# Row maxima into the scores by one-hot products instead of a DMA, and bias loads on a second queue

## The chip, the core and the metric

The kernel runs on one core of a Trainium2 chip. The metric is the device time of one launch in microseconds. TensorE is PE here, VectorE DVE, ScalarE ACT, GpSimd POOL, SyncE SP (its DMA queue SPq).

## What is computed

A pre-norm decoder block over x of shape (16, 128, 128), 16 heads of 8, fp32. Three layers, each over all 16 sequences:

```python
x = x + causal_self_attention(layernorm(x))               # q = k = v, no weights
x = x + cross_attention(layernorm(x), ctx, bias)          # scores = q k^T / sqrt(8) + bias, bias (16, 16, 128, 128)
x = x + attention(hn)                                     # hn = layernorm(x) * g + b, own wq wk wv wo
x = x + top1_moe(layernorm(x) * g2 + b2)                  # 8 experts, hidden 512
```

All softmaxes are over 128 keys of the same sequence.

## The kernel before

**Blocks and slots.** One sequence in one layer is a block: b = 0 to 15 are self attention (SELF), 16 to 31 cross attention (CROSS), 32 to 47 the attention of the last layer (FFN). Two blocks are a pair, q = b // 2. Every engine runs the same loop over slots b with its own part of the work written out by hand, and counting semaphores hold the engines together. After slot 50 comes the routing of rows to experts and the expert stage (from about 490 us on), which the change doesn't touch.

**Scores.** Queries and keys are split into three bf16 parts, and the nine products of parts are stacked in the contraction: 9 x 8 = 72 rows (ROWS). That layout needs another distribution over partitions, so it goes through DRAM: `write_parts(q)` writes q once (192 KB) and k three times (576 KB), `read_stack(q)` waits for those writes and reads both operands back as `stack[:, q % 3]` (2 x 576 KB). For pair q, SP issues the write in slot 2(q-2) and the read in the slot after. The parts come by the chain PE `qk_products` (slot 2q-5), ACT `high_parts`, DVE `first_rest` (same slot), ACT `middle_parts` and POOL `low_parts` (slot 2q-4). ACT takes `middle_parts` after the first exponential of that slot.

**Row maxima.** CROSS and FFN blocks need their row maxima ahead of the exponential. Slot b makes them for block b+2: PE `score_maxes(b+2, g)` (four groups g of four heads) computes plain scores into max_bank, DVE adds the bias (CROSS) and reduces (`row_maxes`), `max_parts` makes two bf16 parts of the negated maxima, high in columns 0 to 15 and the rest of them in 16 to 31. In slot b+1 PE transposes them (`max_transposed`) and DVE copies them out as `maxT[:, b % 2, :]` (`take_maxT`). They enter the scores as two further rows of the contraction (MROWS = 74): the key side of these rows is ones, the query side is maxT, which a DMA puts there:

```python
def max_rows(b):
    wait(sp, s_maxT, b - B + 1)
    sp.dma_start(stack[ROWS:MROWS, b // 2 % NSTACK, 0, :, b % 2 * S:(b % 2 + 1) * S],
                 maxT[0:2 * NH, b % 2, :]).then_inc(s_maxrow[b % 2], 16)
```

**The order on PE in slot b** is: `scores(b, 0)`, `scores(b, 1)`, (FFN: `attention_transposed(b-2)`), `add_outputs(b-1)`, `max_transposed(b+1)`, `score_maxes(b+2, 0)` and `(b+2, 1)`, v products in even slots, `scores(b, 2)`, `out_projected(b-2)`, qk products in odd slots, `scores(b, 3)`, `out_transposed(b-1)`, `score_maxes(b+2, 2)` and `(b+2, 3)`, in even slots `transposes(q+3)`. In a CROSS block a score group is four times a transpose of the bias (fp32, into the bank) and a product on top of it.

**The order on DVE**: in even slots statistics for pair q+3, then `take_maxT(b+1)`, row maxima of groups 0 and 1 of block b+2, values, normalise, residual, `attention(b-1)`, row maxima 2 and 3, `max_parts(b+2)`. POOL computes the inverse deviation for pair q+3 before `low_parts(q+2)` in even slots.

**The order on SP**, all on one DMA queue: odd slots `read_stack(q+2)`, `load_bias(b+4)`, `max_rows(b+1)`; even slots `load_ctx(q+4)`, `load_bias(b+4)`, `max_rows(b+1)`, `write_parts(q+2)`. The biases of blocks 16 to 20 are loaded in slots 5, 7, 9, 11, 13, those of 21 to 31 in slots 17 to 27. From slot 33 on an expert weight (256 KB) goes with each slot, and a filler of 1 MB follows the writes in slots 34, 38 and 42.

Of the kernel before, what the change touches and what calls it, by code (L numbers as in the profile page):

```python
# [7 lines left out]
B, S, D = 16, 128, 128  # L8
NH, HD = 16, 8
# [4 lines left out]
G = 4  # L14
NG = NH // G
PAIR = 2 * S
NT = 3
ROWS = NT * NT * HD
MROWS = ROWS + 2
VC = 32  # L20
VS = 16
MASKED = -1e30
# [36 lines left out]
def build(nc, a, out):  # L59
# [4 lines left out]
    with ctx:  # L64
        def sb(name, shape, dt=f32):
            return ctx.enter_context(nc.sbuf_tensor(name, shape, dt))
# [15 lines left out]
        hT = sb("hT", [128, 2, PAIR])  # L82
        rest = sb("rest", [128, 2, PAIR])
        parts = sb("parts", [128, 2, NT, 2, PAIR], bf16)
        stack = sb("stack", [MROWS, NSTACK, 2, NH, PAIR], bf16)
        vaug = sb("vaug", [128, NVAUG, NH + 1, VS])
        bias_in = sb("bias_in", [128, NBIAS, NH, S])
        probs = sb("probs", [128, 2, NG, G * S])
# [8 lines left out]
        ident = sb("ident", [128, 128])  # L97
        identb = sb("identb", [128, 128], bf16)
        causal = sb("causal", [128, G, S], bf16)
        ones_row = sb("ones_row", [128, PAIR], bf16)  # L100
        zero = sb("zero", [128, 1])
        minus_half = sb("minus_half", [128, 4])
        in_block = sb("in_block", [128, TQ])
# [56 lines left out]
        s_bias = [sem(f"bias_loaded{i}") for i in range(NBIAS)]  # L160
        s_wr = [sem(f"scratch_written{i}") for i in range(2)]
        s_stack = [sem(f"stack_loaded{i}") for i in range(NSTACK)]
        s_ones = sem("ones_in_stack")
        s_maxrow = [sem(f"max_rows_in_stack{i}") for i in range(2)]
        s_pool_const = sem("pool_constants")
        s_ident = sem("identity_causal_zeros")
        s_dve_const = sem("dve_constants")
# [75 lines left out]
        def _(sp):  # L243
# [24 lines left out]
                                ap=[[row_elems, ROWS], [1, row_elems]])  # L268
                sp.dma_start(stack[0:ROWS, i, 1, :, :], k_src).then_inc(s_stack[i], 16)  # L269

            def max_rows(b):
                wait(sp, s_maxT, b - B + 1)
                sp.dma_start(stack[ROWS:MROWS, b // 2 % NSTACK, 0, :, b % 2 * S:(b % 2 + 1) * S],
                             maxT[0:2 * NH, b % 2, :]).then_inc(s_maxrow[b % 2], 16)

            def load_bias(b):
                i = b % NBIAS
                if b - NBIAS >= FIRST_CROSS:
                    sp.wait_ge(s_e, NG * (b - NBIAS + 1))
                sp.dma_start(bias_in[:, i, :, :],  # L280
                             a["bias"][b - B].rearrange("h q k -> q h k")).then_inc(s_bias[i], 16)

            def load_ctx(q):
                i, n = q % 2, 2 * q - B
                if q - 2 >= CROSS_PAIR:
# [39 lines left out]
            for b in range(NB + 1):  # L325
                q = b // 2
                if b % 2 == 1 and q + 2 < NP:
                    read_stack(q + 2)
                if 1 <= b <= 5:
                    load_weights(3 * b - 3, 3 * b)  # L330
                if b == 6:
                    sp.wait_ge(s_pool_const, 1)
                    for i in range(NSTACK):
                        sp.dma_start(stack[ROWS:MROWS, i, 1, :, :],
                                     ones_row[0:2, :].unsqueeze(1).to_broadcast([2, NH, PAIR])).then_inc(s_ones, 16)
                if b % 2 == 0 and CROSS_PAIR <= q + 4 < FFN_PAIR:
                    load_ctx(q + 4)
                if b in BIAS_AT:
                    load_bias(BIAS_AT[b])
                elif 17 <= b and b + 4 < FIRST_FFN:  # L340
                    load_bias(b + 4)
                if FIRST_CROSS <= b + 1 < NB:
                    max_rows(b + 1)
                if b % 2 == 0 and q + 2 < NP:
                    write_parts(q + 2)
                if b > FIRST_FFN:
                    load_expert(b)
                if b in (34, 38, 42):
                    write_filler((b - 34) // 4)
# [25 lines left out]
        def _(pool):  # L375
# [77 lines left out]
            low_parts(1)  # L453
            self_values(1)
            self_values(2)
            nc.gpsimd.memset(ones_row[:], 1.0).then_inc(s_pool_const, 1)
            nc.gpsimd.memset(in_block[:], 1.0).then_inc(s_pool_const, 1)
            nc.gpsimd.memset(before[:], 1.0).then_inc(s_pool_const, 1)
            nc.gpsimd.memset(filler[:], 0.0).then_inc(s_pool_const, 1)
# [1 line left out]
            def constants():  # L461
                pool.wait_ge(s_pool_const, 4)
                nc.gpsimd.affine_select(out=in_block[:], in_=in_block[:], compare_op=ALU.is_ge, fill=0.0, base=0,
                                        pattern=[[-TR, TQ]], channel_multiplier=1).then_inc(s_pool_const, 1)
                nc.gpsimd.affine_select(out=before[:], in_=before[:], compare_op=ALU.is_gt, fill=0.0, base=0,
                                        pattern=[[1, 128]], channel_multiplier=-1).then_inc(s_pool_const, 1)
                pool.wait_ge(s_pool_const, 6)
                nc.gpsimd.affine_select(out=in_block[:], in_=in_block[:], compare_op=ALU.is_ge, fill=0.0, base=TR - 1,
                                        pattern=[[TR, TQ]], channel_multiplier=-1).then_inc(s_pool_const, 1)
                nc.gpsimd.iota(expert_no[:], pattern=[[1, E]], base=0, channel_multiplier=0,  # L470
                               allow_small_or_imprecise_dtypes=True).then_inc(s_pool_const, 1)
                nc.gpsimd.iota(tile_ends[:], pattern=[[TILE, B]], base=0, channel_multiplier=0,
                               allow_small_or_imprecise_dtypes=True).then_inc(s_pool_const, 1)
                nc.gpsimd.iota(tile_no[:], pattern=[[1, NTILES]], base=0, channel_multiplier=0,
                               allow_small_or_imprecise_dtypes=True).then_inc(s_pool_const, 1)
                nc.gpsimd.iota(filler[:].bitcast(i32)[:, 2 * D:WIDTH], pattern=[[0, 1]], base=B * S,
                               channel_multiplier=1).then_inc(s_pool_const, 1)
                nc.gpsimd.iota(rows_out[:].bitcast(i32)[:, :, 2 * D], pattern=[[S, B]], base=0,
                               channel_multiplier=1).then_inc(s_pool_const, 1)

            for b in range(LAST_SLOT):
                q = b // 2
# [39 lines left out]
        def _(pe):  # L522
# [67 lines left out]

            def scores(b, g):
                i, s, bk, kind = b // 2 % NSTACK, b % 2, sbk[g % 2], layer(b)
                depth = ROWS if kind == SELF else MROWS
                wait(pe, s_p, NG * b + g - 1)
                if g == 0:
                    pe.wait_ge(s_stack[i], READS * (b // 2 // NSTACK + 1))
                    if kind == CROSS:
                        pe.wait_ge(s_bias[b % NBIAS], 16 * ((b - B) // NBIAS + 1))
                    if kind != SELF:
                        pe.wait_ge(s_maxrow[b % 2], 16 * ((b - B) // 2 + 1))  # L600
                    if b == FIRST_CROSS:
                        pe.wait_ge(s_ones, 16 * NSTACK)
                if kind == SELF:
                    mm(bk[:], identb[:], causal[:].rearrange("p g k -> p (g k)"), stop=False)
                for h in range(G):
                    o, head = bk[:, h * S:(h + 1) * S], g * G + h
                    if kind == CROSS:
                        tr(o, bias_in[:, b % NBIAS, head, :], stop=False)
                    last = mm(o, stack[0:depth, i, 1, head, s * S:(s + 1) * S],
                              stack[0:depth, i, 0, head, s * S:(s + 1) * S], start=kind == FFN,  # L610
                              stop=kind != SELF or h == G - 1)
                last.then_inc(s_e, 1)

            def add_outputs(b):
# [127 lines left out]
        def _(act):  # L742
# [42 lines left out]
            def take_hn2T(j):  # L785
                act.wait_ge(s_t, NP + j + 1)
                nc.scalar.activation(hn2T[:, j % 2, :], pb[:, 0:PAIR], ACT.Identity,
                                     bias=cols[:, 7:8], scale=cols[:, 6:7]).then_inc(s_hn2, 1)

            high_parts(0)  # L790
            middle_parts(0)
            high_parts(1)
# [3 lines left out]
            for b in range(LAST_SLOT):  # L796
                q = b // 2
                if b < NB:
                    exponentials(b, 0)
                if b % 2 == 0 and q + 2 < NP:  # L800
                    middle_parts(q + 2)
                if FIRST_FFN <= b - 2 < NB:
                    take_attT(b - 2)
                if b < NB:
                    exponentials(b, 1)
                if 0 <= b - 1 < NB:
                    take_out(b - 1)
                if b < NB:
                    exponentials(b, 2)
                if b % 2 == 1 and CROSS_PAIR <= q + 3 < NP:  # L810
                    high_parts(q + 3)
                if b < NB:
                    exponentials(b, 3)
                if b % 2 == 0 and q + 3 < NP:
                    if player(q + 3) == SELF:
                        high_parts(q + 3)
                    else:
                        take_hT(q + 3)
                if b in LAST_NORMS:
                    take_hn2T(LAST_NORMS[b])  # L820
# [27 lines left out]
        def _(dve):  # L848
# [92 lines left out]

            def take_maxT(b):
                dve.wait_ge(s_mtr, b - B + 1)
                wait(dve, s_maxrow[b % 2], 16 * ((b - B) // 2))
                nc.vector.tensor_copy(maxT[:, b % 2, :], fb[:].bitcast(bf16)[:, 0:128]).then_inc(s_maxT, 1)  # L945

            def attention(b):
# [212 lines left out]
```

## Time and profile before

| | |
|---|---|
| time, median of 3 runs | 578.4 us (578.15 to 583.85) |
| profiled execution, its time | 579.91 us |
| profiled execution, its span | 578.2 us |
| granted clock of TensorE, mean | 0.812 of 2.4 GHz |
| PE busy | 373.3 us (65%) |
| DVE, ACT, POOL busy | 291.0, 202.9, 169.9 us |
| moved by DMA | 82.35 MB, mean 142 GB/s |

The span runs from the first to the last instruction on the core. A busy share is an average over stages with different limits: self attention up to about 146 us, cross attention up to about 336, the last attention layer up to about 480, then routing and experts.

### The profile page before, as it was taken

What the parts mean: (1) busy time and instruction counts of PE and PEld (TensorE: products, weight loads), DVE (VectorE), ACT (ScalarE), POOL (GpSimd) and SP (SyncE); (2) the same over time, 40 slices, a digit from 0 to 9 for tenths busy, and PEclk for the clock granted to TensorE, in tenths of its full rate; (3) what the DMA queues carried; (4) which work ended last, traced back from release to release, by engine and by line L of the source; (5) the groups of instructions that cost most, each with busy time, mean ns of one, the idle gap of its engine ahead of it and who ended that gap; (6) DMA issues with size and microseconds to landing.
All of it is one profiled execution on the core that took longest, in us unless ns stands there. A gap on an engine that the chain in (4) does not pass through costs nothing.

```text
span 578.2 us, 11981 instructions
## 1 busy us (share of the span) xinstructions
PE 373.3 (65%) x4299; PEld 318.1 (55%) x4299; DVE 291.0 (50%) x845; ACT 202.9 (35%) x414; POOL 169.9 (29%) x244
## 2 busy tenths in 40 slices
PE   1285666625849696686958966486367395007995
PEld 0164444514638585675857856376356384007995
DVE  4124121215775575755757655545366274404773
ACT  1255444422324232332324333344245163003552
POOL 4222101210122222333334544123123123371543
PEclk9989777777787897987979977857788588557999
DMA  2777677888384856758544433945856421122331
GB/s 76 187 191 201 173 196 214 217 217 215 99 202 128 214 139 174 199 135 217 130 105 116 116 81 103 227 108 131 203 158 156 103 84 47 36 104 68 100 88 39
DMA packets 75335, 82.35 MB, mean 142 GB/s; under 512 B 6171, under 2 KB 61566, under 8 KB 71822
## 3 DMA queue, kind: packets, MB, share of 16 engines
q1 hardware_dynamic: 73774, 78.43, 52.8%
q0 software_dynamic: 1504, 3.16, 1.6%
q8 instruction: 35, 0.57, 0.4%
q14 instruction: 22, 0.18, 0.1%
HBM read 56.20 MB, written 25.51 MB: 141 GB/s over the span
## 4 chain that ended last, share of the span: by engine, by line
DMA 36%; PE 25%; SPq 18%; DVE 10%; issue 5%; POOL 4%; ACT 0%; POOLq 0%; DVEq 0%; ACTq 0%
DMA stack<-maxT 21%; DMA k_scratch<-parts 12%; PE out_bank L524 7%; PE score_bank L524 5%; SPq L257 5%; PE proj_bank L524 4%; PE score_bank L527 3%; PE max_bank L524 3%; SPq L287 3%; POOL routed_rows L507 3%; SPq L266 2%; DVE biased L920 2%; DVE rowmax L924 2%; SPq L253 2%; SPq L269 2%
## 5 line engine op out<-in xcount | busy, mean ns | idle before, releaser
L773 ACT ACTIVATE probs<-score_bank 128x512 f32<-128x512 f32 x192 | 112.2, 598 | 220.4 <-PE score_bank L524 218.7
L524 PE MATMUL score_bank<-stack 74*128 74x128 bf16 (+1 forms) x768 | 111.2, 247 | 49.8 <-DMA stack<-maxT 49.8
L524 PEld LDWEIGHTS score_bank<-stack 74*128 74x128 bf16 (+1 forms) x768 | 74.3, 113 | 64.9 <-issue 57.4
L527 PE MATMUL score_bank<-ident,bias_in 128*128 128x128 f32 x256 | 57.6, 309 | 35.9 <-DMA stack<-maxT 35.9
L524 PE MATMUL out_bank<-probs,vaug 128*32 128x128 f32 x1536 | 68.9, 336 | 0.0
L527 PEld LDWEIGHTS score_bank<-ident,bias_in 128*128 128x128 f32 x256 | 41.1, 161 | 42.1 <-issue 36.1
L429 POOL TENSOR_TENSOR att_sel<-att,in_block 128x1024 f32<-128x1024 f32 x16 | 34.3, 2144 | 89.7 <-DVE att L956 89.7
L524 PEld LDWEIGHTS out_bank<-probs,vaug 128*32 128x32 f32 x1536 | 50.6, 134 | 10.4 <-issue 5.0
L524 PE MATMUL score_bank<-causal,identb 128*128 128x512 bf16 x64 | 29.8, 465 | 40.9 <-DMA stack<-k_scratch 40.9
L381 POOL TENSOR_SCALAR vareps<-meanvar 128x2 f32<-128x2 f32 x32 | 7.1, 223 | 164.4 <-DVE meanvar L869 164.3
L945 DVE COPY maxT<-finish_bank 128x128 bf16<-128x128 bf16 x32 | 7.1, 222 | 93.4 <-PE finish_bank L589 93.4
L920 DVE TENSOR_TENSOR biased<-max_bank,bias_in 128x512 f32<-128x512 f32 x64 | 43.7, 683 | 18.0 <-PE max_bank L524 17.0
L524 PE MATMUL max_bank<-stack 72*128 72x128 bf16 x512 | 44.7, 237 | 12.2 <-DMA stack<-k_scratch 12.2
L950 DVE RECIPROCAL rowsum_inv<-finish_bank 128x16 f32<-128x16 f32 x48 | 12.2, 255 | 68.0 <-PE finish_bank L527 68.0
L924 DVE TENSOR_REDUCE rowmax<-biased 128x4 f32<-128x512 f32 x64 | 43.9, 686 | 2.2
L394 POOL TENSOR_TENSOR parts<-rest,parts 128x512 bf16<-128x512 f32 (+1 forms) x24 | 23.9, 995 | 70.5 <-ACT parts L768 70.5
L524 PEld LDWEIGHTS max_bank<-stack 72*128 72x128 bf16 x512 | 37.0, 107 | 13.2 <-DMA stack<-k_scratch 12.7
L929 DVE TENSOR_REDUCE rowmax<-max_bank 128x4 f32<-128x512 f32 x64 | 41.5, 682 | 1.6 <-PE max_bank L524 1.4
L779 ACT COPY outT<-out_bank 128x512 f32<-128x512 f32 x48 | 28.1, 586 | 29.1 <-PE out_bank L524 29.0
L524 PEld LDWEIGHTS score_bank<-causal,identb 128*128 128x128 bf16 x64 | 7.0, 109 | 46.3 <-issue 44.9
L514 POOL DMA_INDIRECT out<-vaug x23 | 22.6, 982 | 32.4 <-DVE vaug L1120 30.4
L524 PE MATMUL proj_bank<-wxo,att_sel 128*128 128x128 f32 x256 | 32.0, 278 | 0.0
(141 smaller groups left out, 642.5 us busy)
## 6 DMA issues: line engine op xcount, KB each, us to landing
k_scratch<-parts SPq DMA_DIRECT2D x72, 192.0 KB, 3.2
stack<-q_scratch SPq DMA_DIRECT2D x24, 576.0 KB
stack<-k_scratch SPq DMA_DIRECT2D x24, 576.0 KB
q_scratch<-parts SPq DMA_DIRECT2D x24, 192.0 KB, 2.9
bias_in<-in_w SPq DMA_DIRECT2D x16, 256.0 KB, 3.9
routed_rows<-filler SPq DMA_DIRECT2D x2, 1028.0 KB, 8.9
vaug<-routed_rows SPq DMA_DIRECT2D x23, 64.5 KB, 1.8
parts<-routed_rows SPq DMA_DIRECT2D x23, 64.0 KB, 2.1
```

The source lines that it names most:

```text
L257: sp.dma_start(k_rows, parts[:, i, part, wk, :].unsqueeze(1).to_broadcast([128, NT, PAIR])).then_inc(s_wr[i], 16)
L287: sp.dma_start(ctx_in[:, i, :, :], a["ctx"][n:n + 2].rearrange("b s d -> s b d")).then_inc(s_ctx[i], 16)
L394: nc.gpsimd.tensor_tensor(parts[:, i, 2, 0:n, :], rest[:, 0:n, :], parts[:, i, 1, 0:n, :], ALU.subtract).then_inc(s_lo, 1)
L429: nc.gpsimd.tensor_tensor(att_sel[:], att[:, b % 2, :].rearrange("p (h d) -> p d h", d=HD).unsqueeze(3).to_broadcast([128, HD, NH, TQ]), i ...
L514: nc.gpsimd.indirect_dma_start(out=out.rearrange("b s d -> (b s) d"), out_offset=bass.IndirectOffsetOnAxis(ap=tile_res[:, buf, :].bitcast( ...
L524: return nc.tensor.matmul(o, lhsT, rhs, start=start, stop=stop, **kw)
L527: return nc.tensor.matmul(o, src, ident[:], start=True, stop=stop, is_transpose=True)
L773: nc.scalar.activation(probs[:, b % 2, g, :], sbk[g % 2][:], ACT.Exp, scale=1.0 if layer(b) == CROSS else SCALE).then_inc(s_p, 1)
L779: nc.scalar.copy(outT[:], ob[:]).then_inc(s_out, 1)
L920: nc.vector.tensor_tensor(biased[:, u % 2, :], bk[:], bias_in[:, b % NBIAS, g * G:(g + 1) * G, :].rearrange("p h k -> p (h k)"), ALU.add). ...
L924: nc.vector.tensor_reduce(rowmax[:, g * G:(g + 1) * G], biased[:, u % 2, :].rearrange("p (h k) -> p h k", h=G), AX.X, ALU.max).then_inc(s_ ...
L929: nc.vector.tensor_reduce(rowmax[:, g * G:(g + 1) * G], bk[:].rearrange("p (h k) -> p h k", h=G), AX.X, ALU.max).then_inc(s_mfree, 1)
```

## The change

The two further rows leave the stack, and with them `max_rows`, the ones, and their semaphores. A constant `pick` (bf16, 128 x 16 x 128) has ones in rows h and 16 + h of head h. A product of `pick[:, head, :]` with `maxT` (contraction over 128) adds both parts of the negated maxima of that head to every key; it follows each score product of CROSS and FFN blocks, 16 to a block. PE now waits for maxT itself. DVE's copy of maxT, which waited for the DMA, now waits for the scores of the block two before, the last readers of its buffer. The bias loads move from SP to ACT, in the same slots, behind the slot's first exponential.

```diff
-MROWS = ROWS + 2
-        stack = sb("stack", [MROWS, NSTACK, 2, NH, PAIR], bf16)
+        stack = sb("stack", [ROWS, NSTACK, 2, NH, PAIR], bf16)
-        ones_row = sb("ones_row", [128, PAIR], bf16)
+        pick = sb("pick", [128, NH, S], bf16)
...
@@ sync: max_rows, load_bias, the ones and their calls go
-                if b == 6:
-                    sp.wait_ge(s_pool_const, 1)
-                    for i in range(NSTACK):
-                        sp.dma_start(stack[ROWS:MROWS, i, 1, :, :],
-                                     ones_row[0:2, :].unsqueeze(1).to_broadcast([2, NH, PAIR])).then_inc(s_ones, 16)
-                if b in BIAS_AT:
-                    load_bias(BIAS_AT[b])
-                elif 17 <= b and b + 4 < FIRST_FFN:
-                    load_bias(b + 4)
-                if FIRST_CROSS <= b + 1 < NB:
-                    max_rows(b + 1)
@@ gpsimd
-            nc.gpsimd.memset(ones_row[:], 1.0).then_inc(s_pool_const, 1)
+            nc.gpsimd.memset(pick[:], 0.0).then_inc(s_pool_const, 1)
...
+                nc.gpsimd.affine_select(out=pick[:], in_=pick[:], compare_op=ALU.not_equal, fill=1.0, base=0,
+                                        pattern=[[-1, NH], [0, S]], channel_multiplier=1).then_inc(s_pool_const, 1)
+                pool.wait_ge(s_pool_const, 13)
+                nc.gpsimd.affine_select(out=pick[:], in_=pick[:], compare_op=ALU.not_equal, fill=1.0, base=-NH,
+                                        pattern=[[-1, NH], [0, S]], channel_multiplier=1).then_inc(s_pool_const, 1)
@@ tensor, scores(b, g)
                     if kind != SELF:
-                        pe.wait_ge(s_maxrow[b % 2], 16 * ((b - B) // 2 + 1))
+                        pe.wait_ge(s_maxT, b - B + 1)
                     if b == FIRST_CROSS:
-                        pe.wait_ge(s_ones, 16 * NSTACK)
+                        pe.wait_ge(s_pool_const, 14)
...
-                    last = mm(o, stack[0:depth, i, 1, head, s * S:(s + 1) * S],
-                              stack[0:depth, i, 0, head, s * S:(s + 1) * S], start=kind == FFN,
-                              stop=kind != SELF or h == G - 1)
+                    last = mm(o, stack[:, i, 1, head, s * S:(s + 1) * S], stack[:, i, 0, head, s * S:(s + 1) * S],
+                              start=kind == FFN, stop=kind == SELF and h == G - 1)
+                    if kind != SELF:
+                        last = mm(o, pick[:, head, :], maxT[:, b % 2, :], start=False)
@@ scalar, in slot b behind exponentials(b, 0)
+            def load_bias(b):
+                i = b % NBIAS
+                if b - NBIAS >= FIRST_CROSS:
+                    act.wait_ge(s_e, NG * (b - NBIAS + 1))
+                nc.scalar.dma_start(bias_in[:, i, :, :],
+                             a["bias"][b - B].rearrange("h q k -> q h k")).then_inc(s_bias[i], 16)
...
+                if b in BIAS_AT:
+                    load_bias(BIAS_AT[b])
+                elif 17 <= b and b + 4 < FIRST_FFN:
+                    load_bias(b + 4)
@@ vector, take_maxT(b)
-                wait(dve, s_maxrow[b % 2], 16 * ((b - B) // 2))
+                wait(dve, s_e, NG * (b - 1))
```

## Rows read from the trace of the kernel before

**Rows 1.** The chain that ended last, from the page: shares of the span

```profile
DMA stack<-maxT 21%; DMA k_scratch<-parts 12%; PE out_bank L524 7%; PE score_bank L524 5%; SPq L257 5%; PE proj_bank L524 4%; PE score_bank L527 3%; PE max_bank L524 3%; SPq L287 3%; POOL routed_rows L507 3%; SPq L266 2%; DVE biased L920 2%; DVE rowmax L924 2%; SPq L253 2%; SPq L269 2%
```

**Rows 2.** Who waited for whom: us in total, times, longest

```profile
PE score_bank L524 <- DMA stack<-maxT: 49.8, 7, 10.9
PE score_bank L527 <- DMA stack<-maxT: 35.9, 8, 6.7
```

**Rows 3.** Busy time in windows: us; PE, PEld, DVE, ACT, POOL; PEclk, DMA share, GB/s

```profile
90.00:96.00 6.00, 5.18 (x58) 3.78 (x59) 0.02 (x1) 2.87 (x6) 1.50 (x3) 0.64 1.02 282
102.00:116.50 14.50, 10.89 (x121) 8.18 (x122) 2.84 (x12) 6.29 (x12) 2.96 (x5) 0.76 0.81 215
222.70:246.90 24.20, 18.40 (x214) 16.18 (x214) 15.77 (x38) 7.77 (x14) 7.26 (x8) 0.85 0.69 174
396.50:417.40 20.90, 11.68 (x154) 10.15 (x154) 10.03 (x30) 7.56 (x16) 5.65 (x9) 0.74 0.68 166
```

**Rows 4.** SP's issues in a cross pair: start us, us, engine, line

```profile
235.36 0.78 SPq L280 DMA_DIRECT2D bias_in<-in_bias  x1
236.78 5.57 SPq L273 DMA_DIRECT2D stack<-maxT  x1
```

**Rows 5.** PE at the start of a cross pair; in brackets the idle time before

```profile
246.99 0.45 PE L527 MATMUL score_bank<-ident,bias_in 128*128 128x128 f32 x1 [5.05 <-DMA stack<-maxT]
```

**Rows 6.** SP's issues in an FFN pair: write_parts, read_stack

```profile
421.86 0.60 SPq L253 DMA_DIRECT2D q_scratch<-parts  x1
...
426.75 0.85 SPq L266 DMA_DIRECT2D stack<-q_scratch  x1
```

**Rows 7.** PE in FFN pairs, in order of time

```profile
399.76 1.06 PE L524 MATMUL max_bank<-stack 72*128 72x128 bf16 x8
...
417.52 1.01 PE L524 MATMUL score_bank<-stack 74*128 74x128 bf16 x8 [9.15 <-DMA stack<-maxT]
...
435.01 1.01 PE L524 MATMUL score_bank<-stack 74*128 74x128 bf16 x8 [5.95 <-DMA stack<-maxT]
```

**Rows 8.** Low parts, statistics and inverse deviation in FFN pairs

```profile
398.46 1.16 POOL L394 TENSOR_TENSOR parts<-rest,parts 128x512 bf16<-128x512 f32 x1 [1.36 <-ACT parts L768]
...
410.87 0.49 DVE L865 BATCH_NORM_STATS2 stats<-x_sb 128x6 f32<-128x128 f32 x2
...
412.30 1.04 POOL L387 TENSOR_TENSOR rstd<-vareps,minus_half 128x4 f32<-128x4 f32 x1
```

**Rows 9.** SP's issues in the self stage: two read_stack, one load_ctx

```profile
38.20 0.80 SPq L266 DMA_DIRECT2D stack<-q_scratch  x1
...
50.46 0.80 SPq L266 DMA_DIRECT2D stack<-q_scratch  x1
...
99.60 5.46 SPq L287 DMA_DIRECT2D ctx_in<-in_ctx  x1
```

**Rows 10.** PE from a cross pair to the first FFN pair

```profile
299.61 0.61 PE L524 MATMUL max_bank<-stack 72*128 72x128 bf16 x8
...
308.11 0.23 PE L589 MATMUL finish_bank<-identb,maxparts 128*128 128x128 bf16 x1 [0.66 <-DVE maxparts L938]
...
317.95 0.61 PE L524 MATMUL max_bank<-stack 72*128 72x128 bf16 x8
...
339.04 1.06 PE L524 MATMUL max_bank<-stack 72*128 72x128 bf16 x8
```

**Rows 11.** PE, first score_maxes of slot 44, the last with a stack read before it

```profile
460.09 1.06 PE L524 MATMUL max_bank<-stack 72*128 72x128 bf16 x8
```

**Rows 12.** PE from slot 15 into slot 16

```profile
146.27 0.61 PE L524 MATMUL max_bank<-stack 72*128 72x128 bf16 x8
149.41 0.45 PE L527 MATMUL score_bank<-ident,bias_in 128*128 128x128 f32 x1 [2.52 <-DMA stack<-maxT]
...
154.08 1.06 PE L524 MATMUL max_bank<-stack 72*128 72x128 bf16 x8
```

**Rows 13.** A select of 512 columns on POOL, from the groups by line

```profile
L446 POOL TENSOR_SCALAR_AFFINE_SELECT causal<-causal 128x512 bf16<-128x512 bf16 x1 | 0.6, 638 | 0.0
```

More of the change, by code:

```diff
@@ L162, in build @@
         s_stack = [sem(f"stack_loaded{i}") for i in range(NSTACK)]
-        s_ones = sem("ones_in_stack")
-        s_maxrow = [sem(f"max_rows_in_stack{i}") for i in range(2)]
         s_pool_const = sem("pool_constants")
@@ L269, in read_stack @@
                 sp.dma_start(stack[0:ROWS, i, 1, :, :], k_src).then_inc(s_stack[i], 16)
[L271 to L281, printed above, removed]
             def load_ctx(q):
@@ L592, in scores @@
                 i, s, bk, kind = b // 2 % NSTACK, b % 2, sbk[g % 2], layer(b)
-                depth = ROWS if kind == SELF else MROWS
                 wait(pe, s_p, NG * b + g - 1)
```

## The prediction

> **What bounds the kernel now.** I read the chain that ended last first. A fifth of the span is a transfer of 8 KB, the row maxima on their way into the score operand [rows 1]. The list of waits puts 85.7 us of idle PE on it [rows 2]. PE has no other large wait after 150 us, so the middle 300 us are not bound by PE's work: in a cross pair of 24.2 us PE is busy 18.4, DVE 15.8, ACT 7.8; in an FFN pair of 20.9 us 11.7, 10.0 and 7.6 [rows 3].
>
> Why 8 KB takes so long is seen in SyncE's order. In an odd slot SyncE issues the two stack reads (1,152 KB), the bias load (1,024 KB: 16 x 128 x 128 in fp32), and then the row maxima; issuing those alone took 5.57 us, and PE's scores of the next pair began at 246.99, 10.2 us after the issue began [rows 4, 5]. The rows lie behind 2.1 MB of the same queue. The transfer that PE really waits for is the stack read; the wait is charged to whatever stands last in the queue.
>
> The stack read closes a loop. `scores` of the even slot need the row maxima; they let PE reach `max_transposed`; DVE copies maxT; SyncE, which waits for that copy, only then issues `write_parts`; the written parts are read back as the next stack; behind that come the next row maxima. In an FFN pair: write issued 421.86, read issued 426.75, PE released at 435.01 [rows 6, 7]. Every pair goes round this loop once.
>
> **Removed: the row-max DMA and its waits.** Three things change. PE's first scores of a pair need only maxT, which DVE copied a slot earlier. The stack that PE waited for at the slot's start is now needed first at `score_maxes(b+2, 0)`, after two score groups and the values products. And `write_parts` is no longer queued behind a wait for maxT: it goes when its parts are ready. That makes the loop two pairs long, since the parts of pair q+2 depend on slot 2q's first exponential, and their stack is needed a pair later, behind work that no longer waits for it.
>
> FFN pair, the new loop. From `score_maxes` of the even slot (399.76) to DVE's statistics at the next pair's start (410.87) is 11.1 us [rows 7, 8]; the added products (below) make it 12.0. To the end of the deviation 2.5 (413.34), low parts 1.2, write to read 4.9, read to landed at most 8.3 [rows 6 to 8]: 28.9 us, for two pairs, so 14.5 each. Checked from the queue alone: in the self stage, with nothing to wait for but data, reads follow reads after 12.3 us (38.20 to 50.46) [rows 9]; an FFN pair adds 0.5 MB of expert weights where that one had 0.4 MB of others, and at most 2.4 us, so 12.3 to 14.7. The PE and DVE cycle would allow 12.0. I take 14.5. Three of the six pairs also carry 1 MB of filler, 4.8 us at the 215 GB/s of the self stage [rows 3]; part runs while SyncE waits for the write, I charge three quarters: +1.8 on the mean, 16.3. Six pairs: 98 us, against 121.05 now (339.04 to 460.09) [rows 10, 11]: -23.
>
> Cross pair. One pair without a stack wait in it is there: `score_maxes` at 299.61 to that at 317.95, 18.3 us [rows 10]. It is a cycle of two engines: PE's outputs to DVE, DVE's row maxima back to PE. With the products 19.2. The bytes are a second bound: 768 KB written, 1,152 read, two biases of 1,024, ctx 128, together 4.2 MB; at the self stage's 215 GB/s 19.5 us, at the 282 GB/s of one 6 us window 14.9 [rows 3]. With two bounds this close I take 20.0 for the six pairs that load biases and 19.2 for the last two: 158.4 us, against 184.96 now (154.08 to 339.04) [rows 10, 12]: -26.6.
>
> Entry. PE ended slot 15 at 146.9 and sat until 149.41. It could go on at once. From there to `score_maxes` it took 4.7 us, cold after a wait; at up to twice the clock and with 0.45 of new products about 3.0, so `score_maxes` at 149.9 instead of 154.08 [rows 12]: -4.
>
> **Added: 512 one-hot products.** A like product is a score product: bf16, 128 columns. Eight max_bank products with their weight loads take 0.61 us at 2.4 GHz and 1.06 at 1.2 GHz [rows 10]; the level doubles eight spacings, so one is 0.45 / 8 = 56 ns. Sixteen per block are 0.9 us, 29 in all. Groups 2 and 3 of a block lie on the PE to DVE cycle: 0.45 a slot, 0.9 a pair, counted above. Groups 0 and 1 run while DVE ends the row maxima, where PE now waits 0.66 us [rows 10], which covers 0.45; without that cover the pair takes 0.9 more. After 460.09 fourteen groups are left and little waits: +3 us. The bounds are 56 ns and twice that at the 1.2 GHz level; a PE that waits less is granted the higher clock more (0.85 and 0.74 in the rows of a cross and an FFN pair [rows 3]), so I take 56. The Trainium skill, "TensorE: Matmul & The Clock Gate", section "Back-to-back issue gap", gives about 81 ns for sustained pairs of weight load and matmul at 128 columns; the row has 56 for such pairs. By that figure the added work would be 41 us in place of 29 and the result some 4 us later.
>
> **Moved: the bias loads, to ACT.** SyncE loses 16 issues of about 0.8 us, and what is behind them: in the self stage ctx issues took 5.4 us right behind a bias [rows 9], and the writes then stood behind 1.1 MB. On a second queue the write and the bias run side by side. The self stage moves 3.1 MB in a pair of 14.5 us, 215 GB/s; its gaps between write and read would be filled. Lower bound of the gain nothing (that rate is the limit), upper 8 us over five pairs; I take 4, as windows reach 282. ACT pays 0.8 us an issue, behind the first exponential. Queued behind it are `middle_parts`, the second exponential, and behind those POOL's low parts and PE's `scores(b, 3)`. ACT is busy 7.8 of 24.2 us, so this is covered; without cover it is 16 times 0.8, 13 us.
>
> Also removed: three DMAs of ones, in the shadow of the bias load before them. Added on POOL: a memset and two selects of 2,048 columns; the select of 512 took 638 ns [rows 13], so 2.6 us each by size, in slot 2, on the engine that is busy for 170 of 578 us. `take_maxT` waits for scores two blocks back, which PE has behind it. All nothing.
>
> **Sum.** -4 (self) -4 (entry) -26.6 (cross) -23 (FFN) +3 (tail) = -54.6; 578.2 less that is 523.6, and 1.7 us lie around the span in the profiled run (579.91): 525. The profiled run is 1.5 above the median of 578.4, no more than noise.
>
> **Rivals.** *Contention.* With biases in a queue of their own, the read that PE waits for shares the engines with 1 MB that used to stand behind it. A read of 1.15 MB lands after 8.3 us without a bias; two streams at 215 GB/s in all take 10 us. Then a cross pair is about 22.5, the self stage gains nothing: 525 + 15 + 4 = 544. For it: cross bytes need 19.5 us at that rate. Against: 282 GB/s. The Trainium skill, "DMA: Bandwidth & Descriptors", "Rules for kernel authors", says that spreading DMAs over engines doesn't bring bandwidth; the row of 215 GB/s over a self pair is in line with it, this rival is what it would do here.
>
> *The wait only moves.* If the loop stays one pair long, because parts are not ready before the stack has come, an FFN pair is today's 17.5 (417.5 to 435.0) less 0.8 that the write goes earlier, plus 1.8 of filler: 18.5; a cross pair some 21.5. That is 13 and 9 us more: 547. For it: DVE's order puts the statistics behind all row maxima. Against: the sum of 28.9 has that in it.
>
> *Better than that.* FFN pairs at the engines' 12.0 plus 1.8, cross at 19.2: 525 - 14 - 5 = 506.
>
> *Slower.* ACT blocks in its DMA issue as SyncE did, for 5.5 us [rows 4, 9], and with it the exponentials. If all 16 were exposed, 88 us: 613. It takes the gain away from 3.4 us exposed at each issue on. Against: SyncE was held by what it issued right behind a bias; ACT issues one a slot, near 10 us apart, and has 16 us of idle time a pair.
>
> **Chances.** Forecast (515 to 536) 0.46; contention 0.17; the wait only moves 0.18; better 0.12; ACT blocked 0.05; something else 0.02. The range, 504 to 552, takes in the first four. One per cent is about what a measurement of this kernel can tell. Faster by over 1% 0.94, within 1% 0.02, slower 0.04.
>
> **What will show it.** No score product waits for the row maxima; PE's remaining waits are for the stack, at the max_bank products; from `score_maxes` to `score_maxes` cross pairs of about 20 us and FFN pairs of about 16; write issued before maxT is copied; PE's granted clock over 0.85 in cross pairs; ACT's bias issues near 0.8 us. Wrong if these issues take several us, if reads in cross take over 12 us to land, or if each FFN write comes right after a stack has landed.

## The result and the profile after

The changed kernel takes 545.39 us, the median of four runs (543.7 to 553.3), against 581.12 for the kernel before in the same comparison. The ratio is 0.941, 95% interval 0.934 to 0.949: 6% faster, within the range of 504 to 552, but 20 us above the 525 that were forecast and outside the forecast's own band of 515 to 536. 544 is what the contention rival gave, and 547 what the rival gave by which the wait only moves. The time says nothing yet of its reason.

The first profiled execution of the changed kernel was itself disturbed (553.3 us). The profile read here is that of its second measurement, on another chip (549.62 us, span 547.6), where its median was 547.8 and that of the kernel before 578.46. Who waited for whom (us in total, times, longest), PE's and SP's large waits:

```profile
PE max_bank L504 <- DMA stack<-k_scratch: 42.1, 8, 11.9
PE score_bank L504 <- DMA stack<-k_scratch: 38.8, 8, 11.2
...
SPq L250 <- POOL parts L368: 173.6, 15, 17.2
SPq L263 <- DMA k_scratch<-parts: 97.3, 24, 9.6
```

The 85.7 us behind the row maxima are gone [rows 2]. PE now waits for the stack itself, at the max_bank products: 42.1 us, of which 11.9 are in the self stage and 30.2 behind it. The 38.8 us at the score_bank are all in the self stage and no news: before they were 40.9. SP, which used to wait for maxT, waits for parts. Both are what the forecast said they would be. The page of the same execution: busy time, the granted clock in 40 slices, and the products' own group.

```profile
PE 384.4 (70%) x4796; PEld 341.3 (62%) x4811; DVE 292.6 (53%) x845; ACT 206.1 (38%) x430; POOL 175.2 (32%) x246
...
PEclk9989757777798999799799999869699696558999
```

```profile
L504 PE MATMUL score_bank<-maxT,pick 128*128 128x128 bf16 x512 | 95.0, 227 | 0.0
```

The 227 ns are one product's duration from end to end, and they overlap; what one adds to the time is the experiment's to say.

For the comparison I take the marks of the forecast, the first `score_maxes` of slots 16, 32 and 44, which cut the span in four. In the changed kernel, in the timeline of PE:

```profile
154.83 0.61 PE L504 MATMUL max_bank<-stack 72*128 72x128 bf16 x8
...
321.96 0.61 PE L504 MATMUL max_bank<-stack 72*128 72x128 bf16 x8
...
427.20 1.01 PE L504 MATMUL max_bank<-stack 72*128 72x128 bf16 x8 [7.12 <-DMA stack<-k_scratch]
```

| us | before [rows 10 to 12] | forecast | changed |
|---|---|---|---|
| to slot 16 | 154.1 | 146.1 | 154.8 |
| slot 16 to 32, cross | 185.0 | 158.4 | 167.1 |
| slot 32 to 44, FFN | 121.0 | 98 | 105.2 |
| from slot 44 on | 118.1 | 121.1 | 120.4 |
| span | 578.2 | 523.6 | 547.6 |

So the gain is where it was put, and the first three stretches fell short of the forecast, by 8.7, 8.7 and 7.2 us.

### The profile page after: what moved, and what is told of

It reads as the page before. It is cut to its first block, busy times and chain, and to the rows that moved or that the text cites. A ratio compares the mean times of both kernels' runs of the same rounds, so it can differ in the third digit from the quotient of the medians.

```text
span 551.5 us, 12976 instructions
## 1 busy us (share of the span) xinstructions
PE 384.9 (70%) x4811; PEld 338.9 (61%) x4811; DVE 292.0 (53%) x845; ACT 205.7 (37%) x430; POOL 175.3 (32%) x246
## 4 chain that ended last, share of the span: by engine, by line
DMA 31%; PE 24%; SPq 13%; DVE 13%; issue 10%; POOL 7%; DVEq 1%; ACT 0%; POOLq 0%; ACTq 0%
DMA k_scratch<-parts 15%; DMA stack<-k_scratch 14%; SPq L254 6%; PE score_bank L504 6%; PE proj_bank L504 5%; PE max_bank L504 3%; PE prep_bank L504 3%; POOL routed_rows L487 3%; DVE biased L911 2%; SPq L263 2%; DVE rowmax L915 2%; PE score_bank L507 2%; PE finish_bank L507 2%; PE out_bank L504 2%; SPq L250 2%
## 5 line engine op out<-in xcount | busy, mean ns | idle before, releaser
L504 PE MATMUL score_bank<-stack 72*128 72x128 bf16 x768 | 125.3, 235 | 0.0
L504 PE MATMUL score_bank<-maxT,pick 128*128 128x128 bf16 x512 | 94.6, 226 | 0.0
L504 PEld LDWEIGHTS score_bank<-stack 72*128 72x128 bf16 x768 | 77.0, 107 | 12.8 <-issue 6.6
L504 PE MATMUL max_bank<-stack 72*128 72x128 bf16 x512 | 43.4, 234 | 45.1 <-DMA stack<-k_scratch 45.1
L507 PE MATMUL score_bank<-ident,bias_in 128*128 128x128 f32 x256 | 63.4, 283 | 0.0
L504 PE MATMUL out_bank<-probs,vaug 128*32 128x128 f32 x1536 | 57.0, 294 | 0.0
L504 PEld LDWEIGHTS score_bank<-maxT,pick 128*128 128x128 bf16 x512 | 52.5, 102 | 4.7
L504 PEld LDWEIGHTS out_bank<-probs,vaug 128*32 128x32 f32 x1536 | 42.4, 117 | 6.5 <-ACT probs L753 1.2
L507 PEld LDWEIGHTS score_bank<-ident,bias_in 128*128 128x128 f32 x256 | 37.1, 145 | 0.2
L504 PE MATMUL proj_bank<-wxo,att_sel 128*128 128x128 f32 x256 | 34.5, 292 | 0.0
L759 ACT COPY outT<-out_bank 128x512 f32<-128x512 f32 x48 | 28.0, 584 | 15.6 <-PE out_bank L504 15.5
```

The source lines that it names most:

```text
L504: return nc.tensor.matmul(o, lhsT, rhs, start=start, stop=stop, **kw)
L507: return nc.tensor.matmul(o, src, ident[:], start=True, stop=stop, is_transpose=True)
L759: nc.scalar.copy(outT[:], ob[:]).then_inc(s_out, 1)
```

## The experiments

**Which half of the change does it?** The changed kernel again, each part of it alone, and POOL's order swapped.

> The changed kernel once more, beside the three variants. Every theory: 0.94 of the kernel before. What it settles is the self stage: if the second queue itself slows it, its stack reads come again 6 us late by slot 13 (132.3 against 126.0 us); if that was a disturbance of one execution, they come at 126.

Median 547.8 us (544.88 to 549.62) against 578.46: 0.950, interval 0.937 to 0.962. The stack read of slot 13 came at 129.2 us, between the 126.0 of before and the 132.3 of the first profile. The other runs settle it better than this one: in the three others with the bias loads on ACT at these places (the queue alone, low parts first, small bias loads, all below) it came at 132.2, 131.6 and 131.5, in the five with products and the loads on SP's queue at 127.2 to 130.4. So the loads on ACT at these places cost the self stage about 3 us on the mean, and single profiles scatter by as much.

> Products in, bias loads back on SyncE's queue at their old places. Theory 1, the read that PE waits for is slowed by the bias beside it (13 to 15 us from issue to landing in place of 8): with the bias behind the read in one queue the reads land within 9 us and a cross pair falls from 21.8 to about 20, 0.92 of before. Theory 2, the moved queue is what brings the gain in the cross stage: the writes stand behind the bias again and a cross pair is 23 or more, 0.96. Theory 3, neither matters since PE and DVE set the pace: 0.94.

```diff
...
@@ sync, between load_ctx and write_parts
+                if b in BIAS_AT:
+                    load_bias(BIAS_AT[b])
+                elif 17 <= b and b + 4 < FIRST_FFN:
+                    load_bias(b + 4)
@@ scalar
-                if b in BIAS_AT:
...
```

532.39 us (531.82 to 532.81), 0.924 of before (0.913 to 0.936), and 15 us under the changed kernel on the same chip, the ranges of the two far apart. With the products in, the half of the change that moves the bias loads costs 15 us. The marks:

```profile
153.90 0.61 PE L515 MATMUL max_bank<-stack 72*128 72x128 bf16 x8
...
229.92 0.61 PE L515 MATMUL max_bank<-stack 72*128 72x128 bf16 x8
...
249.43 0.61 PE L515 MATMUL max_bank<-stack 72*128 72x128 bf16 x8
...
305.58 0.61 PE L515 MATMUL max_bank<-stack 72*128 72x128 bf16 x8
...
409.36 1.01 PE L515 MATMUL max_bank<-stack 72*128 72x128 bf16 x8 [6.93 <-DMA stack<-k_scratch]
```

The cross stage takes 151.7 us in place of 167.1. Four of its eight pairs are 19.5 us (one is 229.92 to 249.43), two 19.3, the first and the last 17.4 and 17.6, with no wait for a stack in any of them. That is the PE and DVE cycle, forecast at 19.2. The reads of the six pairs with biases landed within 9.9 to 11.1 us of their issue, since PE did not wait for them. Theory 1 stands, theory 2 falls.

> The kernel before with only the bias loads moved to ACT's queue; the row maxima still go by DMA. Theory 1: the maxima no longer stand behind 1 MB, but the stack read is slower by about as much: 0.98 to 1.01. Theory 2: the five microseconds of bias ahead of the maxima are saved in six pairs, 0.95. FFN pairs stay at 20 us in both.

```diff
@@ kernel before: load_bias from sync to scalar, behind exponentials(b, 0)
-                if b in BIAS_AT:
...
+                if b in BIAS_AT:
...
```

579.12 us (574.36 to 582.26), 1.003 of before (0.998 to 1.008). Alone the second queue brings nothing: the six cross pairs with biases gain 4.7 us together, as the row maxima no longer stand behind 1 MB, and slot 16's `score_maxes` comes 4.2 us later (158.3). The time is within theory 1; the 5 us a pair of theory 2 did not come.

> The changed kernel with POOL's low parts ahead of the inverse deviation in even slots, so that the parts are written 2 to 3 us earlier. If the loop over two pairs (parts, write, read) sets the pace, a pair gets 1 us shorter from the cross stage on: 0.92. If contention or the PE and DVE cycle does, nothing: 0.94.

```diff
-                    if q + 3 < NP:
-                        inverse_deviation(q + 3)
                     if q + 2 < NP:
                         low_parts(q + 2)
+                    if q + 3 < NP:
+                        inverse_deviation(q + 3)
```

539.31 us (536.18 to 540.02), 0.935 (0.923 to 0.947), 8.5 us under the changed kernel. The bias loads are still on ACT's queue, and yet no cross pair waits for its stack; most of them take 19.9 us, the cross stage 158.0. So the wait that the bias beside the read causes has a second condition, the loop of parts: with the parts written earlier the late read is still in time. The read also goes ahead of the bias here (200.51 against 201.91 us), so the two conditions are not told apart. The FFN stage gained less, 101.6 in place of 105.2.

That a pair is 19.9 and not the 19.5 of products only is seen at DVE's `max_parts`, which POOL's low parts now run beside:

```profile
213.13 1.15 POOL L368 TENSOR_TENSOR parts<-rest,parts 128x512 bf16<-128x512 f32 x1 [0.60 <-ACT parts L748]
213.75 0.56 DVE L927 TENSOR_SCALAR maxparts<-rowmax 128x16 bf16<-128x16 f32 x1
214.58 0.23 PE L569 MATMUL finish_bank<-identb,maxparts 128*128 128x128 bf16 x1 [1.59 <-DVE maxparts L929]
```

In products only the same DVE instruction takes 0.17 us at that place, ahead of the low parts, and PE's wait is 1.21: both are 0.4 us shorter, as the pair is.

**Is it the bytes, the issue on ACT, or the moment?**

> The changed kernel, bias loads on ACT's queue in the same slots, but those of blocks 21 to 31 load one head of sixteen (64 KB), so these blocks compute with older bias data for the other heads. The issues and their places stay, the bytes go. Theory 1, bytes beside the read are what slows the cross stage: no bias bytes, a cross pair at 19.2 as with the loads on SyncE's queue, reads landing in 8 us; 0.92 to 0.93 of before. Theory 2, the DMA issue on ACT ahead of middle parts and second exponential is what costs: a pair stays at 21.5, 0.945.

```diff
-                nc.scalar.dma_start(bias_in[:, i, :, :],
-                             a["bias"][b - B].rearrange("h q k -> q h k")).then_inc(s_bias[i], 16)
+                n = 1 if b > 20 else NH
+                nc.scalar.dma_start(bias_in[:, i, 0:n, :],
+                             a["bias"][b - B][0:n].rearrange("h q k -> q h k")).then_inc(s_bias[i], 16)
```

This kernel leaves out fifteen heads of sixteen of the biases of blocks 21 to 31, and its output is wrong by that. 531.93 us (528.21 to 535.02), 0.921 (0.912 to 0.930). Four cross pairs are 19.5 us, no pair waits for a stack, the stage is 151.1. ACT issues as often and at the same places, 0.34 us each in place of 0.69, and that costs nothing. It is the bytes.

> The changed kernel, bias loads still on ACT's queue, but behind the fourth exponential of the slot instead of the first, 7 to 8 us later. The bytes and the queue stay; only what they lie beside changes: the odd slot's load is issued when the stack read is nearly in. If the overlap with the read is what costs, a cross pair is 19 to 20 us and the whole 0.925 to 0.935 of before; if two queues at once are slow wherever they meet, it stays at 21.5 us and 0.945, or the write is late instead of the read.

```diff
                 if b < NB:
-                    exponentials(b, 0)
-                if b in BIAS_AT:
...
+                    exponentials(b, 3)
+                if b in BIAS_AT:
...
```

534.27 us (531.75 to 535.74), 0.932 (0.926 to 0.939). All bytes on the second queue, but each load later in its slot: the cross stage takes 154.0 us, two short waits are left (0.65 and 0.35). Each issue in this stage takes ACT 0.69 or 0.70 us, as in the changed kernel. So neither the second queue, nor ACT's issue, nor the sum of bytes is the cost; it is what they lie beside. In the changed kernel a bias load is issued 1 us ahead of the read that PE needs next, and the next bias before that read is in. SP's and ACT's issues, and PE:

```profile
204.78 0.69 ACTq L774 DMA_DIRECT2D bias_in<-in_bias  x1
...
214.02 0.69 ACTq L774 DMA_DIRECT2D bias_in<-in_bias  x1
```

```profile
205.76 0.81 SPq L263 DMA_DIRECT2D stack<-q_scratch  x1
...
219.94 0.56 SPq L250 DMA_DIRECT2D q_scratch<-parts  x1
```

```profile
218.77 1.01 PE L504 MATMUL max_bank<-stack 72*128 72x128 bf16 x8 [1.47 <-DMA stack<-k_scratch]
```

The read takes 13.0 us from issue to PE's start (13.6 and 14.1 at the two other waits of this stage), against the 9.9 to 11.1 at most of products only; in the kernel before it was at most 8.3 in an FFN pair without a filler [rows 6, 7]. A wait of 1.5 us doesn't look like much. What follows it is in the windows: the read's flight and the stretch behind the wait in the changed kernel, then a whole pair of products only (us; PE, PEld, DVE, ACT, POOL; PEclk, DMA share, GB/s).

```profile
205.80:218.80 13.00, 10.09 (x155) 8.99 (x145) 9.10 (x24) 5.25 (x11) 3.85 (x6) 0.97 0.89 218
218.80:225.20 6.40, 6.40 (x40) 6.15 (x41) 3.57 (x8) 0.60 (x1) 1.11 (x1) 0.53 0.83 218
```

```profile
219.30:238.70 19.40, 17.95 (x250) 16.80 (x246) 15.44 (x39) 7.78 (x14) 7.07 (x8) 1.00 0.83 211
```

Behind the wait PE was granted 0.53, that is the lower of its two levels for nearly all of 6.4 us, with PE busy the whole time. The pair that starts at 218.77 has no stack wait in it and takes 22.3 us (to 241.11, its successor's mark), 2.8 more than the 19.5 of products only, which ran at 1.00. The windows of the two pairs, first the changed kernel's:

```profile
218.77:241.11 22.34, 20.90 (x246) 19.41 (x247) 15.14 (x35) 7.78 (x16) 6.28 (x6) 0.87 0.69 182
```

```profile
210.39:229.92 19.53, 18.08 (x248) 16.80 (x248) 15.57 (x40) 7.78 (x14) 7.20 (x7) 1.00 0.82 211
```

PE is idle for the same 1.4 us in both and has the same work but for two records; the 2.8 us are all busy time, at a granted 0.87. So the waits of the cross stage, 4.24, 1.47 and 2.08, are 7.8 us, and six pairs took 130.3 against 114.8. The rest, 7.7 us, is what the pairs behind the three waits took more (2.0, 2.8 and 3.0), all three with a granted clock of 0.86 to 0.90. That it is the clock rests on these rows and was not tried by itself. The pair of products only also shows that 211 GB/s over a whole pair leaves no wait: the engines of the DMA were not short of bandwidth in the mean.

**What do the products cost?** Twice as many in half of the groups, the new ones with zeros.

> Products only, and in groups 0 and 1 of each cross and FFN block every one-hot product is followed by one with zeros: 256 more products, 14.3 us at 56 ns. Theory A, they run while DVE ends the row maxima, where PE still waits 0.24 us in even and 1.21 us in odd slots: 0.2 us a pair, 3 us in all. Theory B, PE is the bound: 14 us, 0.949.

> The same in groups 2 and 3, which lie between the row maxima's transpose and the outputs' transpose, on the PE to DVE cycle: 0.45 us a slot where that cycle is the bound, 8 cross pairs 7 us, the tail 2, FFN pairs nothing if the queue bounds them: 9 to 14 us, 0.940 to 0.949. Theory C, they are covered as well: 0.924.

```diff
-                        last = mm(o, pick[:, head, :], maxT[:, b % 2, :], start=False)
+                        last = mm(o, pick[:, head, :], maxT[:, b % 2, :], start=False, stop=g not in (2, 3))
+                        if g in (2, 3):
+                            last = mm(o, pick[:, head, :], zeros[:], start=False)
```

Both are products only with these products added. Groups 0 and 1: 536.77 us (532.19 to 540.33), 0.924 (0.913 to 0.934). Groups 2 and 3: 541.51 us (538.14 to 547.87), 0.938 (0.928 to 0.948). Products only was 0.924 in its own comparison. The totals scatter; the pairs don't. A cross pair is 19.5 us without them, 19.6 with more in groups 0 and 1, 20.4 with more in 2 and 3. PE's transposes of the maxima, with what they waited for, in the first and in the second kernel:

```profile
234.17 0.23 PE L582 MATMUL finish_bank<-identb,maxparts 128*128 128x128 bf16 x1 [0.76 <-DVE maxparts L933]
243.62 0.23 PE L582 MATMUL finish_bank<-identb,maxparts 128*128 128x128 bf16 x1
253.81 0.23 PE L582 MATMUL finish_bank<-identb,maxparts 128*128 128x128 bf16 x1 [0.76 <-DVE maxparts L933]
```

```profile
225.00 0.23 PE L582 MATMUL finish_bank<-identb,maxparts 128*128 128x128 bf16 x1 [0.24 <-DVE maxparts L933]
235.66 0.23 PE L582 MATMUL finish_bank<-identb,maxparts 128*128 128x128 bf16 x1 [1.21 <-DVE maxparts L933]
245.43 0.23 PE L582 MATMUL finish_bank<-identb,maxparts 128*128 128x128 bf16 x1 [0.24 <-DVE maxparts L933]
```

In the second kernel, as in products only, PE waits 0.24 and 1.21 us for DVE here. Eight more products ahead of that wait eat 0.45 of it: 0.76 are left of 1.21, nothing of 0.24. Behind it they are paid in full: sixteen a pair, 0.9 us, 56 ns each. Theory A stands for the cross pairs, and so does the bound of groups 2 and 3. In the FFN stage, for which nothing was expected, the marks give 107.2 us with more in groups 0 and 1 and 109.7 with more in 2 and 3, against 103.8. Why was not tried; the second is from the longest of its four executions.

**What bounds the FFN pairs?**

> Products only (bias loads on SyncE), and the three 1 MB fillers written in slots 28, 30 and 32 instead of 34, 38 and 42: two of them while cross pairs are bound by PE and DVE and the queue has no bias. If the queue's bytes set the pace of the FFN pairs, as forecast (filler 1.8 us of 16.3 on the mean), the six pairs take 94 in place of 100 us: 0.914 against 0.924. If PE and DVE do, or the loop of parts, nothing changes.

```diff
-                if b in (34, 38, 42):
-                    write_filler((b - 34) // 4)
+                if b in (28, 30, 32):
+                    write_filler((b - 28) // 2)
```

This is products only with the fillers moved. 524.85 us (515.77 to 528.92), 0.917 (0.909 to 0.925) against 0.924: the intervals overlap. By the marks the FFN stage takes 96.9 us against 103.8 of products only, as the first theory had it (6 us); the cross stage, which now carries the fillers, takes 1.5 more. In the changed kernel the large stack waits, at slots 36, 40 and 44 (5.07, 8.19, 7.12), are those of the pairs with a filler. One of them:

```profile
376.39 0.56 SPq L250 DMA_DIRECT2D q_scratch<-parts  x1
...
379.72 1.25 SPq L287 DMA_DIRECT2D routed_rows<-filler  x1
...
382.59 0.81 SPq L263 DMA_DIRECT2D stack<-q_scratch  x1
```

```profile
393.97 1.01 PE L504 MATMUL max_bank<-stack 72*128 72x128 bf16 x8 [8.19 <-DMA stack<-k_scratch]
```

Write to read took 6.2 and read to landed 11.4 us, where the forecast had 4.9 and 8.3.

> Products, bias loads on SyncE's queue, fillers in slots 28, 30 and 32, and POOL's low parts ahead of the inverse deviation. The cross pairs are bound by PE and DVE, so low parts first gives nothing there; in FFN pairs the loop of parts and the queue are close, half a microsecond a pair: 0.908 to 0.916 of before, 3 to 5 us under products only.

Products only with the diffs of the filler and of low parts first.

521.89 us (518.47 to 524.61), 0.908 (0.902 to 0.913): the lowest median here, though its interval overlaps that of the fillers alone. The last mark:

```profile
400.45 1.01 PE L515 MATMUL max_bank<-stack 72*128 72x128 bf16 x8 [2.79 <-DMA stack<-k_scratch]
```

From slot 32 (310.50) to it are 90.0 us: low parts first, which brought little in FFN pairs while fillers stood in the queue, brings 7 once they are gone. In the cross stage, where nothing was expected, it costs 5.6 us (157.3 against 151.7): most pairs with biases are 19.9 us again, with PE's wait of 1.59 for the max parts, and one is 21.5 at a granted clock of 0.92.

## Why the prediction was right, and where it was not

**The wait and its loop.** Right. With the products alone the kernel is 46 us faster (578.46 to 532.39). The 85.7 us of waiting are gone, the stack wait came back at the max_bank products, and the loop runs over two pairs: the late reads of the changed kernel's cross stage come in every other pair, and parts written earlier remove their waits.

**The wait only moves.** This rival's 547 is as near to the time as contention's 544, and its cross pair of 21.5 us as near to the 21.7 measured. Its mechanism is excluded all the same. It needs parts that are not ready before the stack has come; in the changed kernel the next write goes out while the read issued at 382.59, for which PE waits until 393.97, is still on its way:

```profile
389.04 0.58 SPq L250 DMA_DIRECT2D q_scratch<-parts  x1
```

And with products only no cross pair waits for a stack at all.

**The cross pair: "I take 20.0 for the six pairs".** This term failed, for the kernel as changed, and the forecast's own sign of being wrong came with it: reads in cross that take over 12 us to land (13.0 to 14.1). The engine cycle was right (19.2 forecast, 19.5 measured), the bytes as a bound were wrong. Their 19.5 us at 215 GB/s are by chance the 19.5 measured at 211 GB/s, but a pair is 19.5 with the bias bytes left out too. For two bounds so close the forecast added 0.5 us a pair (20.0). What happened in its place is the rival's mechanism: the read shares its 13 us with biases. The rival's size was wrong as well: 22.5 a pair were worked out, 21.7 came, and of the 2.6 over products only half is wait and half the longer pair behind a wait, at the lower clock, which neither had priced. That the rival's 544 met the time has some luck in it: its sum had 15 us for the cross pairs, 4 for the self stage and nothing for the FFN pairs, where the cross stage came 8.7 us over the forecast, what lies ahead of it 8.7 and the FFN pairs 7.2.

**Self stage and entry, -4 and -4.** Slot 16's `score_maxes` is at 154.8 against 154.1, so nothing is left of the 8 us. The entry gave 2.5 of its 4: from the last `score_maxes` of slot 15 to the first of slot 16 it takes 5.3 us, 7.8 before [rows 12]. That is the wait of 2.52. The stretch behind it was forecast at 3.0 in place of 4.7 and stayed at 4.7, although the clock rose as forecast; first the changed kernel, then the window of before:

```profile
149.50 0.61 PE L504 MATMUL max_bank<-stack 72*128 72x128 bf16 x8
...
154.74 0.23 PE L569 MATMUL finish_bank<-identb,maxparts 128*128 128x128 bf16 x1 [1.76 <-DVE maxparts L929]
```

```profile
150.10:154.83 4.73, 2.97 (x58) 2.51 (x56) 4.53 (x13) 2.29 (x5) 0.00 (x0) 1.00 0.02 3
```

```profile
149.41:154.08 4.67, 4.67 (x49) 3.46 (x50) 2.59 (x9) 1.70 (x3) 1.77 (x3) 0.50 0.01 4
```

PE does its part in 3.0 us now, but waits 1.76 for DVE's max parts; DVE's work in this stretch is what the forecast had at nothing.

The self stage ended 3.2 us later (149.50 against 146.27), where 4 were to be gained. ACT reached slot 5 sooner than SP had and issued the first bias at 51.73 us, between a read and the weights; SP had issued it at 68.70:

```profile
51.73 0.87 ACTq L774 DMA_DIRECT2D bias_in<-in_bias  x1
```

```profile
57.24 7.76 SPq L254 DMA_DIRECT2D k_scratch<-parts  x3
71.00 0.81 SPq L263 DMA_DIRECT2D stack<-q_scratch  x1
```

That read came 20.0 us behind its predecessor; before it was 15.1. With the biases on SP it is 15.5 to 16.7 in five profiles. Late on ACT's queue it is 18.2, and yet the read of slot 13 came at 126.0 as before and the mark of slot 16 at 151.8. So here too the places of the loads matter and not the second queue as such; which load costs the 3 us was not tried.

**FFN pairs: 14.5 and 1.8.** The mechanism was right, the size 7 us short over six pairs. The run with the fillers moved away separates the two terms. Its six pairs take 96.9 us, 16.1 each, with no filler in the queue: the 14.5 were 1.6 short, near 10 us in all. The fillers were charged too much, 10.8 us where products only lost 6.9 by them. The loop over two pairs in that run:

```profile
325.23 0.61 PE L515 MATMUL max_bank<-stack 72*128 72x128 bf16 x8 [2.27 <-DMA stack<-k_scratch]
...
338.39 0.49 DVE L856 BATCH_NORM_STATS2 stats<-x_sb 128x6 f32<-128x128 f32 x2
...
342.02 0.56 SPq L250 DMA_DIRECT2D q_scratch<-parts  x1
...
348.04 0.80 SPq L263 DMA_DIRECT2D stack<-q_scratch  x1
...
357.10 0.89 PE L515 MATMUL max_bank<-stack 72*128 72x128 bf16 x8 [1.46 <-DMA stack<-k_scratch]
```

`score_maxes` to statistics is 13.2 us (forecast 12.0), to the write 3.6 (3.7), write to read 6.0 (4.9), read to landed 9.1 (8.3): 31.9 in place of 28.9. Three terms, read off single pairs of the kernel before, were each about 1 us small.

**The products.** Right to the digit: 56 ns each where they count, in groups 2 and 3; the cover of groups 0 and 1 is 0.24 and 1.21 us and holds all but 0.2 a pair. The 81 ns of the Trainium skill, "TensorE: Matmul & The Clock Gate", section "Back-to-back issue gap", did not show here: a product paid in full cost 56. The tail was +3 forecast, +2.3 measured.

**The bias loads on ACT.** The issue costs nothing, as forecast (0.69 to 0.87 us each, none blocked), so the slow rival did not come; with the loads late in the slot one of the sixteen did block, for 5.88 us. The gain given for it did not either: it is a loss of 15 us. The Trainium skill, "DMA: Bandwidth & Descriptors", section "Rules for kernel authors", has it that spreading over engines brings no bandwidth: the runs agree (1.003 with the second queue alone). What it costs in latency the runs add.

## What to carry to other kernels

The wait on a small transfer at the end of a queue was here a wait for what lay ahead of it. Taking the small transfer away moved the wait to the big one and paid by as much work as stands between the two places, and more because an issue had been held behind the same wait. On one queue order worked as a priority: with the bulk load behind it the urgent read landed within 9.9 to 11.1 us, with the same load beside it on a second queue it took 13.0 to 14.1, and a load later in the slot was nearly harmless again. Added work was free only ahead of a wait that was already there, and up to its length.

## What was not expected of the hardware

A PE wait of 1.5 us (at the end of 13 us in which PE was busy for 10.1) was followed by 6.4 us with a granted clock of 0.53, while PE was busy throughout; the pair cost 2.8 us more on top of the wait. Over the three waits of this stage the pairs behind them cost as much again as the waits: 7.7 us on 7.8. It does not follow every pause: products only has a wait of 1.2 us in each cross pair and stays at 1.00; with the bias loads late a wait of 0.65 was followed by a pair at 0.92 that took 1.6 more, one of 0.35 by nothing; and in each of the two runs with low parts first one cross pair ran at 0.92 without a stack wait before it (21.3 and 21.5 us).

Two queues moved 218 GB/s while the read took 13.0 us, and one queue 211 GB/s over a pair without any wait for a stack: the rate was nearly the same, and what differed is what went beside the read.

A DVE instruction of 0.17 us (128 x 16, bf16 out) took 0.56 us where a POOL instruction of 1.15 us (128 x 512) ran beside it, and the pair became longer by the difference.
